# Quantising the input of two four-bit feed-forwards inside the stages ahead of them

## Chip, cores and metric

The program runs on one core of one Trainium2 chip, as one launch. The metric is the device time of the execution in microseconds (us); the profile is one execution taken by the hardware profiler. Engines go by PE (TensorE), DVE (VectorE), ACT (ScalarE), POOL (GpSimd) and SP (SyncE).

## What is computed

A stack of layers on a stream `x` of 2 x 1024 tokens with 128 features. The change is about three neighbouring ones. Each normalises its input, and the four-bit feed-forward (layer L2) rounds both factors of each product to a four-bit grid in blocks of 16 numbers:

```
def fp4_quant_dequant(x):                     # blocks of 16 along the last axis
    scale = max(|xb|) / 6 per block, at least 1e-12
    idx = searchsorted(_MID, |xb / scale|)
    return _GRID[idx] * sign(xb) * scale      # grid 0, .5, 1, 1.5, 2, 3, 4, 6
def _L2_ffn_ref(x, w_gate, w_up, w_down):     # 128 -> 352 -> 128
    h = silu(fp4_linear(x, w_gate)) * fp4_linear(x, w_up)
    return fp4_linear(h, w_down)              # fp4_linear rounds input and weight
...
x = x + 0.5 * _L1_ffn_ref(_layernorm(x), ...)     # ternary weights, 128 -> 512 -> 512 -> 512 -> 128
x = x + 0.5 * _L2_ffn_ref(_layernorm(x), ...)
x = x + _L2_attn_ref(_layernorm(x), ...)          # 16 heads, window of 32 keys
x = x + 0.5 * _L2_ffn_ref(_layernorm(x), ...)
```

## The kernel before

Tokens lie on the partitions: 16 tiles of 128 tokens, in four chunks of four tiles. `x` is the stream, `y` a normalised copy, `zt` that copy turned (features on the partitions), which the products read. The list `STAGES` runs one function per stage, each in a block of its own; in a block every engine has a queue written out by hand, and counters (semaphores) tie them. Between blocks all engines meet. Four stages matter here.

**The ternary stage** (`ternary_ffn`, with `four_bit=True`) makes the inner products of all chunks and then, chunk by chunk, the second hidden product (`pe_hidden(1, c)`, L508, closed by a Gelu on ACT, L535) and the output of the chunk before (`pe_down`, L518), which DVE scales and adds to `x` (`dve_add`, L549 and L552).

**The four-bit stage** (`l2_ffn`, run twice) makes its own input, per chunk: statistics on DVE (`dve_spread`, L3065 to L3070), a root on POOL (L3231), the normalisation, on DVE for chunk 0 (L3075) and on ACT for the others (`act_normal`, L3082 and L3087), the scaling to the grid and the exponents on DVE (`dve_x_grid`, L2952 to L2961), a step size on ACT (`act_x_step`, L3199), rounding on DVE (`dve_x_round`, L2967, L2968, L3099), four transposes on PE (`pe_turn_x`, L3160) and a copy to `zt` on ACT (L3203). Then, per tile, `pe_up` makes two products (L3171) into one of two pairs of banks, ACT gates one (`act_gated`, L3211), DVE multiplies (`dve_gated`, L3107), which frees the pair. Four tiles together are the hidden chunk, which DVE brings to the grid (`dve_hidden_grid`, begins with L3120) and rounds (`dve_hidden_round`) before PE turns it and makes the output (L3182, L3192) and DVE adds it (L3113).

**The attention stage** (`l2_attn`) between the two runs a loop over the 16 tiles. For tile n PE makes the scores (`pe_scores`, L3551 and L3556), DVE takes the maximum and subtracts it (`dve_shift`, L3620 and L3624); then PE turns the probabilities of tile n-1, makes the values and starts on the next scores, for which it waits for the subtraction. DVE meanwhile divides tile n-1 (`dve_norm`, L3631 and L3633). In tiles 5, 9 and 13 PE turns a finished chunk (L3520), in 6, 10 and 14 it makes its output (L3533), which DVE adds to `x` (`dve_add`, L3539); the next turn of probabilities waits for that add.

The order of the queues in the four-bit stage's opening is, on DVE and on PE:

```
dve_spread 0, 1; dve_normal 0; dve_x_grid 0; dve_spread 2; dve_x_round 0; dve_x_grid 1; dve_spread 3
dve_x_round 1; dve_x_grid 2; dve_gated 0; dve_x_round 2; dve_gated 1; dve_x_grid 3; dve_gated 2
dve_x_round 3; dve_gated 3; dve_hidden_grid 0 (with dve_gated 4, 5); dve_gated 6, 7; dve_hidden_grid 1
PE: pe_turn_x 0; pe_up 0, 1; pe_turn_x 1; pe_up 2, 3; pe_turn_x 2; pe_up 4, 5; pe_turn_x 3; pe_up 6 to 13
```

## Time and profile before

| | us |
|---|---|
| median of 3 runs | 2329.48 (2328.91 to 2331.28) |
| the profiled execution | 2333.61 |
| its span | 2331.8 |
| PE busy in the span | 2101.2 (90%) |
| DVE busy | 1543.0 (66%) |
| ACT busy | 1197.4 (51%) |

The span is counted from the first to the last instruction, and all times of rows from its start. Busy time is the time in which an engine executed something. A share over the whole span mixes stages with different limits, so the stretch of one stage is looked at by itself. The granted clock of PE is given as a part of 2.4 GHz; 0.50 is 1.2 GHz.

### The profile page before, as it was taken

The page shows a single profiled execution, that of the slowest core. Times are in us where ns is not written, and L with a number is a line of the kernel's source. Part 1 is how long each engine was busy: PE and PEld are TensorE (multiplying, and loading weights), DVE is VectorE, ACT ScalarE, POOL GpSimd, SP SyncE. Part 2 cuts the span into 40 slices and gives each one's busy share as a digit, 9 for nine tenths or more (in the row PEclk, how much of TensorE's full clock was granted, in tenths as well). Part 3 has the DMA queues.
Part 4 walks back from the last instruction along what each step waited for, and adds up shares of the span by engine and source line. Part 5 has one row for each costly group of instructions (what it writes and reads, how often), then busy time and mean ns, then how long its engine had stood idle before and what let it go on. Part 6 is the DMA issues. An engine that isn't in the chain of part 4 may idle for free. (4 is left out here: it accounts for less than half of the span.)

```text
span 2331.8 us, 40476 instructions
## 1 busy us (share of the span) xinstructions
PE 2101.2 (90%) x15567; PEld 1158.7 (50%) x15567; DVE 1543.0 (66%) x2999; ACT 1197.4 (51%) x2168; POOL 530.6 (23%) x896
## 2 busy tenths in 40 slices
PE   6998998796999898899999999989877957999999
PEld 3765665474675576454322222234445725445454
DVE  7996996656997897325678888350297777066650
ACT  4774773254775775222378878632143643242421
POOL 4432430313431441104154544000004010000000
PEclk9999999797999999999989999899978978999999
DMA  4000000001000000002111211000000110000000
GB/s 147 4 6 3 4 5 6 5 3 52 4 5 5 1 7 6 28 0 67 37 54 38 53 49 40 2 10 0 5 1 16 29 52 9 0 1 1 1 9 10
DMA packets 48549, 45.18 MB, mean 19 GB/s; under 512 B 33124, under 2 KB 39460, under 8 KB 47588
## 3 DMA queue, kind: packets, MB, share of 16 engines
q1 hardware_dynamic: 39252, 34.90, 5.0%
q0 software_dynamic: 9104, 7.68, 1.3%
q8 instruction: 125, 2.05, 0.4%
q14 instruction: 68, 0.56, 0.1%
HBM read 34.18 MB, written 4.46 MB: 17 GB/s over the span
## 5 line engine op out<-in xcount | busy, mean ns | idle before, releaser
L2532 DVE TENSOR_REDUCE fa_top<-psum 128x1 f32<-128x1024 f32 x256 | 300.4, 1215 | 53.3 <-PE psum L2411 52.7
L2508 ACT ACTIVATE fa_prob<-psum 128x512 f32<-128x512 f32 x512 | 274.9, 598 | 67.6 <-PE psum L2466 67.2
L758 POOL TENSOR_TENSOR turn_a<-turn_a,turn_b 128x1024 f32<-128x1024 f32 x64 | 151.3, 2364 | 268.5 <-DVE turn_b L978 268.5
L2466 PE MATMUL psum<-fa_stack_q,fa_stack_k 74*128 74x512 bf16 x512 | 160.4, 396 | 7.9 <-ACT fa_prob L2508 5.2
L2481 PE MATMUL psum<-fa_prob,fa_pair_v 128*32 128x512 f32 x1024 | 141.7, 626 | 0.0
L2366 POOL DMA_DIRECT2D area_a<-fa_parts_dram x240 | 133.5, 559 | 18.4 <-issue 18.4
L775 PE MATMUL psum<-area_a,zt 128*128 128x512 f32 x256 | 129.0, 627 | 4.5 <-ACT zt L1193 2.7
L2121 POOL TENSOR_TENSOR rstd<-spread,minus_half 128x4 f32<-128x4 f32 x20 | 20.3, 1014 | 468.3 <-DVE spread L2110 468.3
L2466 PEld LDWEIGHTS psum<-fa_stack_q,fa_stack_k 74*128 74x128 bf16 x512 | 33.8, 98 | 161.4 <-ACT fa_prob L2508 118.7
L3875 PE MATMUL psum<-hidden_a,area_b 128*128 128x512 f32 x256 | 112.5, 592 | 0.0
L3875 PE MATMUL psum<-hidden_b,area_b 128*128 128x512 f32 x256 | 111.5, 592 | 0.0
L3914 DVE TENSOR_TENSOR scaled<-psum,area_b 128x512 f32<-128x512 f32 x8 | 5.5, 692 | 138.4 <-PE psum L3884 138.4
L799 PE MATMUL psum<-ident,qk 128*128 128x128 f32 x512 | 72.3, 286 | 27.3 <-DVE turn_b L978 17.1
L991 DVE TENSOR_TENSOR qk<-turn_a,norm 128x1024 f32<-128x1024 f32 x64 | 78.4, 1225 | 27.9 <-POOL norm L750 26.3
L975 DVE TENSOR_TENSOR turn_a<-psum,direct 128x512 f32<-128x512 f32 x128 | 87.7, 685 | 7.9 <-ACT squares L881 5.9
L834 PE MATMUL psum<-ident,prob 128*128 128x128 f32 x512 | 69.7, 279 | 25.7 <-ACT prob L918 23.5
L834 PEld LDWEIGHTS psum<-ident,prob 128*128 128x128 f32 x512 | 55.4, 141 | 73.9 <-ACT prob L918 71.2
L1111 PE MATMUL psum<-glu_in,area_a 128*128 128x512 f32 (+1 forms) x192 | 88.8, 598 | 3.6 <-ACT glu_in L1098 3.6
L978 DVE TENSOR_TENSOR turn_b<-psum,cross 128x512 f32<-128x512 f32 x128 | 86.9, 679 | 0.0
L775 PEld LDWEIGHTS psum<-area_a,zt 128*128 128x128 f32 x256 | 50.5, 201 | 71.3 <-issue 53.8
L918 ACT ACTIVATE prob<-shifted_scores 128x1024 f32<-128x1024 f32 x64 | 67.6, 1057 | 33.4 <-DVE shifted_scores L1002 33.3
L2409 PE MATMUL psum<-fa_stack_k,fa_stack_q 64*128 64x512 bf16 x256 | 81.5, 385 | 2.8 <-DVE fa_top L2532 2.7
(421 smaller groups left out, 4684.4 us busy)
## 6 DMA issues: line engine op xcount, KB each, us to landing
area_b<-in_L_ffn SPq DMA_DIRECT2D x2, 2888.0 KB, 9.6
fa_stack_q<-fa_parts_dram SPq DMA_DIRECT2D x144, 32.0 KB
fa_stack_k<-fa_parts_dram SPq DMA_DIRECT2D x144, 32.0 KB
area_a<-fa_parts_dram POOLq DMA_DIRECT2D x120, 32.0 KB, 2.7
area_a<-in_L_ffn SPq DMA_DIRECT2D x1, 2482.0 KB, 18.1
moved_halves<-y SPq DMA_DIRECT2D x16, 127.0 KB
area_a<-fa_parts_dram POOLq DMA_DIRECT2D x120, 16.0 KB, 2.5
area_b<-in_L_attn SPq DMA_DIRECT2D x1, 1880.5 KB, 20.4
```

The lines of the kernel that those rows point to most:

```text
L758: nc.gpsimd.tensor_tensor(turn_a[:], turn_a[:], turn_b[:], ALU.add).then_inc(rotary_sums.handle, 1)
L775: nc.tensor.matmul(qk_banks[:, s, :], zt[:, 64 + n * P:64 + (n + 1) * P], wq[:, s * LA_INNER:(s + 1) * LA_INNER], start=True, stop=True).t ...
L834: last = nc.tensor.transpose(heads_of(prob_banks)[:, h, :], prob[:, h, :], core.ident[:])
L975: nc.vector.tensor_tensor(turn_a[:, s * H:(s + 1) * H, :], qk_banks[:, s, :].rearrange("p (h d) -> p h d", d=D), direct[:, s, t:t + 1, :]. ...
L978: last = nc.vector.tensor_tensor(turn_b[:, s * H:(s + 1) * H, :].rearrange("p h (a d) -> p h a d", a=2), partner, cross[:, s, t:t + 1, :]. ...
L1111: last = nc.tensor.matmul(pair(u)[0:rows, part, :], w(f"w1{l}")[:, part * GLU_HID + at:part * GLU_HID + at + rows], ht[:, c * CHUNK:(c + 1 ...
L2366: pool.dma_start(to[at:at + D, :, :], parts_dram[b, which, pair[which]].rearrange("(h d) t -> d h t", d=D)[:, 2 * q:2 * q + 2, tokens]).th ...
L2466: nc.tensor.matmul(slot_bank("scores", n), stack_k[0:STACK, head, t * P:(t + 1) * P], stack_q[0:STACK, head, half * CHUNK:(half + 1) * CHU ...
L2481: last = nc.tensor.matmul(psum[at:at + GROUP, SUM_BANK, :], pair_v[:, g % 2, t, j, :], prob[:, (2 * s + j) % RING, half * CHUNK:(half + 1) ...
L2508: nc.scalar.activation(prob[:, (2 * s + j) % RING, half * CHUNK:(half + 1) * CHUNK], slot_bank("scores", n), ACT.Exp, scale=float(D) ** -0 ...
L2532: nc.vector.tensor_reduce(top[:, g % 2, j, t:t + 1], psum[:, 2 * j:2 * j + 2, :].rearrange("p a n -> p (a n)"), AX.X, ALU.max, negate=True ...
L3875: last = nc.tensor.matmul(hid_bank(n), w(name)[:, e * TF_HID + m * P:e * TF_HID + (m + 1) * P], source[:, i, e, :], start=(e == 0), stop=( ...
```

## The change

A class `FourBitInput` holds the steps that make the four-bit stage's input, so that other stages can issue them. In the ternary stage DVE does the statistics and the normalisation of chunks 0 to 2 behind the adds of these chunks, and also grid and rounding of chunks 0 and 1, which PE turns there and ACT copies to `zt`. In the attention DVE does the same work between tiles (statistics in tiles 7, 11, 15, normalisation in 8, 12 and after 15, grid in 9 and 13, rounding in 10 and 14), but nothing is turned. The four-bit stage (`first_l2_ffn` with `turned=True`, `second_l2_ffn` without) keeps the statistics and normalisation of chunk 3, grid and rounding of chunks 2 and 3 and their turns, and, in its second run, the turns of chunks 0 and 1. Its queues have a new order: the turn of chunk 2 stands ahead of `pe_up(2)`, that of chunk 3 ahead of `pe_up(10)`. The diff, cut:

```diff
+        given = FourBitInput(core, ctx) if four_bit else None
...
         def act_gelu(act, step, c):
             out, scale = ((hb, "t1"), (ha, "t2"))[step]
             for m in range(M):
+                if given is not None and step and c >= 2 and m == 2:
+                    given.act_step(act, c - 2)
                 n = step * HIDS + c * M + m
...
+                if given is not None:
+                    for c in range(given.NORMAL_EARLY):
+                        given.pool_root(pool, c)
...
                     pe_hidden(pe, 1, c)
                     if 0 <= c - 2 < early:
                         following.pe_turn(pe, c - 2, psum[:, c - 2, :])
+                    if given is not None and c >= 2:
+                        if c == 2:
+                            pe.wait_ge(*guest.taken.at(4))
+                        given.pe_turn(pe, c - 2, psum[:, c - 2, :])
                     pe_down(pe, c - 1)
...
+                        if given is not None and step and c >= 2:
+                            given.act_take(act, c - 2, psum[:, c - 2, :])
...
+                    if given is not None and c < given.NORMAL_EARLY:
+                        link = Steps(dve, given.chain)
+                        dve.wait_ge(*added.at(c + 1))
+                        given.dve_spread(dve, link, c)
+                        given.dve_normal(dve, c)
+                        if c < given.EARLY:
+                            given.dve_grid(dve, link, c)
+                            given.dve_round(dve, link, c)
+                        link.close()
...
+class FourBitInput:
+
+
+    EARLY, NORMAL_EARLY = 2, 3
...
+    def dve_spread(self, dve, link, c):
+        core, nc = self.core, self.core.nc
+        for i in self.tiles(c):
+            last = nc.vector.bn_stats(core.stats[:, i, :], core.x[:, i, :])
+        link(last)
+        for i in self.tiles(c):
+            last = nc.vector.bn_aggr(core.moments[:, i, :], core.stats[:, i, :])
+        link(last)
+        nc.vector.tensor_scalar(core.spread[:, self.group(c)], core.moments[:, self.group(c), 1], 1e-5, None,
+                                ALU.add).then_inc(self.spreads.handle, 1)
...
+    def pool_root(self, pool, c):
+        core = self.core
+        pool.wait_ge(*self.spreads.at(c + 1))
+        core.nc.gpsimd.tensor_tensor(core.rstd[:, self.group(c)], core.spread[:, self.group(c)], core.minus_half[:, self.group(c)],
+                                     ALU.pow).then_inc(self.roots.handle, 1)
...
+    def dve_normal(self, dve, c):
+        core, nc = self.core, self.core.nc
+        dve.wait_ge(*self.roots.at(c + 1))
+        for i in self.tiles(c):
+            last = nc.vector.tensor_scalar(core.y[:, i, :], core.x[:, i, :], core.moments[:, i, 0:1], core.rstd[:, i:i + 1],
...
+        last.then_inc(self.whole.handle, 1)
...
+    def dve_grid(self, dve, link, c):
+        dve.wait_ge(*self.whole.at(c + 1))
+        q4_to_grid(self.core.nc, link, self.blocks(self.chunk(c)), self.blocks(self.chunk(c)), self.small[c % 2])
+        q4_exponent(self.core.nc, self.chunk(c), self.x_step[:, c % 2, :]).then_inc(self.exps.handle, 1)
...
+    def act_step(self, act, c):
+        act.wait_ge(*self.exps.at(c + 1))
+        self.core.nc.scalar.activation(self.x_step[:, c % 2, :], self.x_step[:, c % 2, :], ACT.Copy, scale=Q4_MAGIC).then_inc(self.steps.handle, 1)
...
+    def dve_round(self, dve, link, c):
+        dve.wait_ge(*self.steps.at(c + 1))
...
+                                          ALU.mult).then_inc(self.ready.handle, 1)
...
+    def pe_turn(self, pe, c, bank):
+        core, nc = self.core, self.core.nc
+        pe.wait_ge(*self.ready.at(c + 1))
+        for j, i in enumerate(self.tiles(c)):
+            last = nc.tensor.transpose(bank[:, j * P:(j + 1) * P], core.y[:, i, :], core.ident[:])
+        last.then_inc(self.turned.handle, 1)
+
+    def act_take(self, act, c, bank):
+        core, nc = self.core, self.core.nc
+        act.wait_ge(*self.turned.at(c + 1))
+        nc.scalar.copy(core.zt[:, c * CHUNK:(c + 1) * CHUNK], bank).then_inc(self.taken.handle, 1)
...
+def l2_ffn(core, area, turned):
...
-            if c == 1 and j == 0:
+            if c <= 1 and j == 0:
                 pe.wait_ge(*x_taken.at(CHUNKS))
...
-                for c in range(CHUNKS):
-                    pool.wait_ge(*spreads.at(c + 1))
-                    nc.gpsimd.tensor_scalar(minus_mean[:, group(c)], core.moments[:, group(c), 0], -1.0, None, ALU.mult).then_inc(centres.handle, 1)
-                    nc.gpsimd.tensor_tensor(core.rstd[:, group(c)], core.spread[:, group(c)], core.minus_half[:, group(c)],
-                                            ALU.pow).then_inc(roots.handle, 1)
+                pool.wait_ge(*given.spreads.at(CHUNKS))
+                nc.gpsimd.tensor_scalar(minus_mean[:], core.moments[:, group(last_chunk), 0], -1.0, None, ALU.mult).then_inc(centres.handle, 1)
+                given.pool_root(pool, last_chunk)
...
-                for c in range(CHUNKS):
-                    pe_turn_x(pe, c)
-                    if c < 3:
-                        pe_up(pe, 2 * c)
-                        pe_up(pe, 2 * c + 1)
-                for n in range(6, 14):
+                if not turned:
+                    given.pe_turn(pe, 0, psum[:, 4, :])
+                    given.pe_turn(pe, 1, psum[:, 5, :])
+                for n in range(14):
+                    if n == 2:
+                        given.pe_turn(pe, 2, psum[:, 6, :])
+                    if n == 10:
+                        given.pe_turn(pe, 3, psum[:, 7, :])
                     pe_up(pe, n)
...
-                act_normal(act, 1)
-                act_x_step(act, 0)
-                act_normal(act, 2)
-                act_take_x(act, 0)
-                act_x_step(act, 1)
+                if not turned:
+                    given.act_take(act, 0, psum[:, 4, :])
+                    given.act_take(act, 1, psum[:, 5, :])
                 act_gated(act, 0)
-                act_normal(act, 3)
-                act_x_step(act, 2)
-                act_take_x(act, 1)
                 act_gated(act, 1)
+                given.act_step(act, 2)
+                act_normal(act)
                 act_gated(act, 2)
-                act_x_step(act, 3)
-                act_take_x(act, 2)
-                act_gated(act, 3)
-                act_gated(act, 4)
-                act_take_x(act, 3)
-                act_gated(act, 5)
-                act_gated(act, 6)
+                given.act_take(act, 2, psum[:, 6, :])
+                for n in range(3, 8):
+                    act_gated(act, n)
                 act_step(act, 0)
-                act_gated(act, 7)
+                given.act_step(act, 3)
                 act_gated(act, 8)
                 act_gated(act, 9)
+                given.act_take(act, 3, psum[:, 7, :])
                 act_step(act, 1)
                 for n in range(10, 14):
                     act_gated(act, n)
...
-                dve_spread(dve, link, 0)
-                dve_spread(dve, link, 1)
-                dve_normal(dve, link, 0)
-                dve_x_grid(dve, link, 0)
-                dve_spread(dve, link, 2)
-                dve_x_round(dve, link, 0)
-                dve_x_grid(dve, link, 1)
-                dve_spread(dve, link, 3)
-                dve_x_round(dve, link, 1)
-                dve_x_grid(dve, link, 2)
+                given.dve_spread(dve, link, 3)
+                given.dve_grid(dve, link, 2)
                 dve_gated(dve, 0)
-                dve_x_round(dve, link, 2)
                 dve_gated(dve, 1)
-                dve_x_grid(dve, link, 3)
+                given.dve_round(dve, link, 2)
                 dve_gated(dve, 2)
-                dve_x_round(dve, link, 3)
                 dve_gated(dve, 3)
                 dve_hidden_grid(dve, link, 0, (4, 5))
+                given.dve_grid(dve, link, 3)
                 dve_gated(dve, 6)
                 dve_gated(dve, 7)
+                given.dve_round(dve, link, 3)
                 dve_hidden_grid(dve, link, 1, (8, 9))
...
+def first_l2_ffn(core, area):
+    l2_ffn(core, area, turned=True)
+
+
+def second_l2_ffn(core, area):
+    l2_ffn(core, area, turned=False)
...
+                for c in range(given.NORMAL_EARLY):
+                    given.pool_root(pool, c)
...
@@ -3744,6 +3798,8 @@
                         act_take_p(act, n - 1)
                     if n + 1 < TILES:
                         act_take_v(act, n + 1)
+                    if n in (10, 14):
+                        given.act_step(act, n // PER_CHUNK - 2)
                     act_exp(act, n)
...
+                later = Steps(dve, chain)
                 for n in range(TILES):
                     dve_shift(dve, n)
                     if n:
                         dve_norm(dve, n - 1)
                     if n < CHUNKS:
                         dve_keep(dve, n)
+                    if n in (10, 14):
+                        given.dve_round(dve, later, n // PER_CHUNK - 2)
                     if n > PER_CHUNK and n % PER_CHUNK == 2:
                         dve_add(dve, n // PER_CHUNK - 1)
+                    if n in (7, 11, 15):
+                        dve.wait_ge(*added.at(n // PER_CHUNK))
+                        given.dve_spread(dve, later, n // PER_CHUNK - 1)
+                    if n in (8, 12):
+                        given.dve_normal(dve, n // PER_CHUNK - 2)
+                    if n in (9, 13):
+                        given.dve_grid(dve, later, n // PER_CHUNK - 2)
+                given.dve_normal(dve, 2)
+                later.close()
                 dve_norm(dve, TILES - 1)
                 dve_add(dve, CHUNKS - 1)
...
-          ("L2_ffn", l2_ffn, 0), ("L2_attn", l2_attn, 1), ("L2_ffn", l2_ffn, 0),
+          ("L2_ffn", first_l2_ffn, 0), ("L2_attn", l2_attn, 1), ("L2_ffn", second_l2_ffn, 0),
```

PE, at the end of the ternary stage and the start of the first four-bit stage. Before (L518 outputs, L508 hidden products, L3160 turns of the input, L3171 `pe_up`):

```order
L518 MATMUL psum<-area_b,hidden_a 128x128 x16
L508 MATMUL psum<-hidden_b,area_b 128x512 x16
L518 MATMUL psum<-area_b,hidden_a 128x128 x16
L508 MATMUL psum<-hidden_b,area_b 128x512 x16
L518 MATMUL psum<-area_b,hidden_a 128x128 x32
L554 UNCONDITIONAL_BRANCH
L3234 UNCONDITIONAL_BRANCH
L3160 MATMUL psum<-ident,y 128x128 x4
L3171 MATMUL psum<-area_a,zt 128x352 x4
```

and with the change (L519, L509, L3120 and L3237 are the same four):

```order
L519 MATMUL psum<-area_b,hidden_a 128x128 x16
L509 MATMUL psum<-hidden_b,area_b 128x512 x16
L3120 MATMUL psum<-ident,y 128x128 x4
L519 MATMUL psum<-area_b,hidden_a 128x128 x16
L509 MATMUL psum<-hidden_b,area_b 128x512 x16
L3120 MATMUL psum<-ident,y 128x128 x4
L519 MATMUL psum<-area_b,hidden_a 128x128 x32
L557 UNCONDITIONAL_BRANCH
L3290 UNCONDITIONAL_BRANCH
L3237 MATMUL psum<-area_a,zt 128x352 x4
L3120 MATMUL psum<-ident,y 128x128 x4
```

Two turns now stand ahead of the outputs of chunks 1 and 2 in the ternary stage, and in the four-bit stage one turn stands between tiles 1 and 2, where there were four, the first ahead of all products.

DVE, in the attention loop, tile 10. Before:

```order
L3620 TENSOR_REDUCE wa_top<-psum 128x16
L3624 TENSOR_TENSOR wa_shifted<-psum,wa_top 128x1024
L3631 RECIPROCAL wa_rec<-psum 128x16
L3633 TENSOR_TENSOR wa_tokens<-psum,wa_rec 128x4x4x8
L3539 TENSOR_TENSOR x<-psum,x 128x512
L3620 TENSOR_REDUCE wa_top<-psum 128x16
```

and with the change, from the end of tile 9's guest on (L3672 to L3685 are L3620 to L3633 of before, L3591 is the add L3539):

```order
L2977 TENSOR_TENSOR y<-y,q_x_small_0_143 128x512
L2982 TENSOR_SCALAR q_x_step<-y 128x512
L3672 TENSOR_REDUCE wa_top<-psum 128x16
L3676 TENSOR_TENSOR wa_shifted<-psum,wa_top 128x1024
L3683 RECIPROCAL wa_rec<-psum 128x16
L3685 TENSOR_TENSOR wa_tokens<-psum,wa_rec 128x4x4x8
L2988 SCALAR_TENSOR_TENSOR y<-q_x_step,y 128x512
L2989 SCALAR_TENSOR_TENSOR q_x_step<-q_x_step,y 128x512
L3112 TENSOR_TENSOR y<-q_x_step,q_x_small_0_142 128x512
L3591 TENSOR_TENSOR x<-psum,x 128x512
L3672 TENSOR_REDUCE wa_top<-psum 128x16
```

The grid of chunk 0 stands between tile 9 and the maximum of tile 10, its rounding between tile 10's division and the add.

## Rows read from the trace of the kernel before

**Rows 1.** Windows: start:end, us, then busy us of PE, PEld, DVE, ACT, POOL, clock, DMA.
```profile
1641.30:1682.50 41.20, 38.35 (x162) 22.85 (x160) 5.53 (x8) 5.50 (x8) 0.00 (x1) 1.00 0.01 1
...
1682.50:1710.50 28.00, 14.24 (x32) 8.09 (x32) 26.16 (x80) 14.54 (x36) 7.07 (x10) 0.58 0.03 10
...
1817.10:1873.60 56.50, 50.20 (x1434) 42.81 (x1432) 35.24 (x50) 33.92 (x59) 0.00 (x0) 0.98 0.10 20
...
1874.90:1902.90 28.00, 11.19 (x32) 6.33 (x32) 26.12 (x80) 14.89 (x37) 7.21 (x10) 0.70 0.24 98
```
**Rows 2.** Timeline of DVE, first four-bit stage: start, us, instruction, count, idle before and releaser.
```profile
1682.54 0.87 DVE L3065 BATCH_NORM_STATS2 stats<-x 128x6 f32<-128x128 f32 x4 [1.43 <-PEq L4258]
...
1685.42 1.12 DVE L3075 TENSOR_SCALAR y<-x,moments,rstd 128x128 f32<-128x128 f32 x4
...
1686.58 0.69 DVE L2952 TENSOR_REDUCE q_x_small<-y 128x32 f32<-128x512 f32 x1
...
1689.19 0.86 DVE L3065 BATCH_NORM_STATS2 stats<-x 128x6 f32<-128x128 f32 x4
...
1690.58 0.68 DVE L2967 SCALAR_TENSOR_TENSOR y<-q_x_step,y 128x512 f32<-128x512 f32 x1
...
1692.63 0.68 DVE L2952 TENSOR_REDUCE q_x_small<-y 128x32 f32<-128x512 f32 x1
...
1710.54 1.62 DVE L3120 TENSOR_REDUCE q_small<-q_hidden 128x88 f32<-128x1408 f32 x1
...
1718.62 0.52 DVE L3107 TENSOR_TENSOR q_hidden<-psum,q_gate 128x352 f32<-128x352 f32 x1 [1.36 <-ACT q_gate L3211]
...
1719.18 1.62 DVE L3120 TENSOR_REDUCE q_small<-q_hidden 128x88 f32<-128x1408 f32 x1
```
**Rows 3.** Timeline of POOL, PE and ACT, first four-bit stage.
```profile
1685.70 1.04 POOL L3231 TENSOR_TENSOR rstd<-spread,minus_half 128x4 f32<-128x4 f32 x1
...
1692.77 1.12 PE L3160 MATMUL psum<-ident,y 128*128 128x128 f32 x4 [13.12 <-DVE y L3099]
...
1694.83 5.06 PE L3171 MATMUL psum<-area_a,zt 128*128 128x352 f32 x8 [0.94 <-ACT zt L3203]
...
1695.35 0.63 ACT L3199 ACTIVATE q_x_step<-q_x_step 128x512 f32<-128x512 f32 x1 [0.57 <-DVE q_x_step L2961]
...
1701.85 1.45 PE L3171 MATMUL psum<-area_a,zt 128*128 128x352 f32 x4 [1.16 <-DVE q_hidden L3107]
```
**Rows 4.** Windows in the opening of the first four-bit stage (clock third from the end).
```profile
1686.00:1700.00 14.00, 6.29 (x14) 3.79 (x15) 13.24 (x43) 10.28 (x28) 4.98 (x5) 0.50 0.00 1
...
1700.00:1704.00 4.00, 2.14 (x8) 1.02 (x6) 3.60 (x7) 2.51 (x6) 0.00 (x0) 0.93 0.00 0
...
1704.00:1710.00 6.00, 5.31 (x12) 3.27 (x12) 5.50 (x13) 1.58 (x3) 0.00 (x0) 0.50 0.00 0
```
**Rows 5.** Timeline of PE and DVE, end of the ternary stage.
```profile
1641.30 13.90 PE L508 MATMUL psum<-hidden_b,area_b 128*128 128x512 f32 x32
...
1679.69 0.69 DVE L549 TENSOR_TENSOR scaled<-psum,area_b 128x512 f32<-128x512 f32 x1 [2.16 <-PE psum L518]
```
**Rows 6.** Timeline of PE and DVE, attention loop and its end.
```profile
1819.35 0.66 PE L3520 MATMUL psum<-ident,wa_tokens 128*128 128x128 f32 x4
...
1835.32 1.22 DVE L3620 TENSOR_REDUCE wa_top<-psum 128x16 f32<-128x1024 f32 x1 [1.30 <-PE psum L3556]
...
1839.71 1.22 DVE L3620 TENSOR_REDUCE wa_top<-psum 128x16 f32<-128x1024 f32 x1 [1.34 <-PE psum L3556]
...
1843.19 0.69 DVE L3539 TENSOR_TENSOR x<-psum,x 128x512 f32<-128x512 f32 x1 [0.45 <-PE psum L3533]
...
1844.71 1.22 DVE L3620 TENSOR_REDUCE wa_top<-psum 128x16 f32<-128x1024 f32 x1 [0.82 <-PE psum L3556]
...
1868.95 0.26 DVE L3631 RECIPROCAL wa_rec<-psum 128x16 f32<-128x16 f32 x1 [3.06 <-PE psum L3592]
```
**Rows 7.** Timeline of DVE, second four-bit stage, its second hidden grid.
```profile
1911.56 1.62 DVE L3120 TENSOR_REDUCE q_small<-q_hidden 128x88 f32<-128x1408 f32 x1
```

More of the change, by code:

```diff
@@ L3096, in dve_x_round @@
[L3096 to L3100 removed]
+            last.then_inc(given.whole.handle, 1)
         def dve_gated(dve, n):
```

98 lines of the change are left out of this document (40 added, 58 removed).

## The prediction, made before the changed kernel had run

> **What bounds the kernel now.** I first read the windows, one per stretch of the four stages that the change touches [rows 1]; in each the reader is to see which engine is full. In the last 41.2 us of the ternary feed-forward TensorE is busy for 38.35 us at full clock and VectorE for 5.53: TensorE is the bound and VectorE has room. The opening of the first four-bit stage turns that round: in 28.0 us VectorE is busy for 26.16 and TensorE for 14.24, and the second four-bit stage opens alike (26.12 of 28.0). What ends last there is VectorE's own queue, so work taken out of it shortens the opening until another wait ends last. In the windowed attention both are nearly full (TensorE 50.20, VectorE 35.24 of 56.5 us), so there I went on to the timeline: between tiles VectorE waits 1.34 us for the next scores [rows 6]. That gap is all the free room the guests find there.
>
> **What is taken out of a four-bit stage.** From the starts of VectorE's instructions [rows 2]: the statistics of a chunk take 1.39 us (1689.19 to 1690.58), its normalisation 1.16 (1685.42 to 1686.58), scaling to the grid with the exponents 2.61 (1686.58 to 1689.19), rounding with the last multiply 2.05 (1690.58 to 1692.63). Gone from each stage are three statistics (4.2), one normalisation (1.16), two grids (5.2) and two roundings (4.1): 14.7 us of VectorE's 28. ScalarE loses its normalisation of chunks 1 and 2, which VectorE never waited for.
>
> **What the opening then waits for.** I lay it out anew, counting from VectorE's first instruction. The prices are these [rows 3]: a tile's products take TensorE 2.53 us at the low clock (5.06 for eight instructions, two tiles) and 1.45 at the high one, four transposes 1.12 low (0.66 high [rows 6]), a step on ScalarE 0.63; a gate product on VectorE is 0.56 with its gap [rows 2]. VectorE does chunk 3's statistics and chunk 2's grid up to 4.0. TensorE starts at 0.1, since `zt` is filled, and is cold: tile 0 is made at 2.6, tile 1 at 5.1. ScalarE's gate of tile 1, half a us, ends at 5.65 and VectorE's product at 6.2: a first stall of about 1.1. The step of chunk 2 ends at 6.3, its rounding at 8.35. Only now can TensorE turn chunk 2, and in its queue tiles 2 to 13 stand behind that turn, though tiles 2 and 3 lie in chunk 0 and need nothing of it. So VectorE idles again: transposes to 9.5, tiles 2 and 3 to 14.5, last product over at 15.6 if TensorE stays cold; with the high clock from 8.35 on, 13.0. The hidden grid began at 28.0 before (1710.54) [rows 2].
> From there to the second hidden grid it was 8.64 us, 1.36 of them a wait for ScalarE [rows 2], which the new ScalarE order takes away; chunk 3's grid and rounding are added: 7.28 + 2.61 + 2.05 = 11.94. The second hidden grid begins at 25.0 (warm) or 28.5 (cold, with 1 us for tiles 4 and 5, whose products come every 2.53) instead of 36.64. Later the order is unchanged, and chunk 3's turn, which now stands ahead of tile 10, has its input at that moment, 8 us before the product is wanted: nothing. Gain 8.1 to 11.6; I take **10.0**, since the clock was granted at 0.93 for 4 us and at 0.50 around it [rows 4]: neither end holds throughout.
> The Trainium skill ("TensorE: Matmul & The Clock Gate", section "What's actually happening") says that half clock is the default state and activity releases it; with a pause of 3.3 us ahead of the turn I read it as the cold end for both openings, 2323.1 us, a rival below. The trace sides with it only in part, since there is a high clock in a half idle opening [rows 4].
>
> The **second four-bit stage** has to turn chunks 0 and 1 itself: two turns of 1.12 ahead of tile 0, with the first copy hidden under the second turn. All of the chain above moves back by 2.2 us. Its old opening had the same length (36.66 us from 1874.90, where its window begins, to its second hidden grid at 1911.56) [rows 1, 7]. Gain 5.9 to 9.4; I take **7.9**.
>
> **What the ternary stage pays.** TensorE is the bound there, and gets 2 x 4 transposes, 0.66 each four at full clock [rows 6]: +1.3. The inputs are there in time: between chunk 0's output and its turn stands a hidden product of 13.9 us [rows 5], and the chain on VectorE, add and all (1.4 + 1.4 + 1.1 + 1.2 + 2.6 + 0.7 + 2.1), is 10.5; chunk 1 likewise. ScalarE's steps and copies lie in its gaps between two Gelus. After chunk 2's add VectorE has 2.16 us until chunk 3's product [rows 5]; now 1.39 + 1.04 (root on GpSimd [rows 3]) + 0.1 + 1.16 = 3.7 stand there ahead of chunk 3's product and add, with which the stage ends: +1.5. Together **+2.8** (1.3 if the last part hides, 3.4 with a slower root).
>
> **What the attention pays.** Its loop is a ring: scores on TensorE, maximum and subtraction on VectorE, next scores. Guests stand in VectorE's gap of 1.34 [rows 6]. Statistics (tiles 7, 11) exceed it by 0.06, normalisations (8, 12) fit, grids (9, 13) exceed it by 1.27 each. In tiles 10 and 14 the add leaves 0.45 + 0.82 = 1.27 [rows 6] for a rounding of 2.05, and the add is now late for the turn that waits for its bank: 0.8 each. After tile 15 VectorE waits 3.06 for the values [rows 6]; statistics, root and normalisation are 3.7: +0.6. Sum 0.1 + 2.5 + 1.6 + 0.6 = **+4.8**. Below, 3.1, if only grids and the tail count; above, 9.8, if the two statistics and two normalisations find no gap either (2 x 1.39 + 2 x 1.16). I stay with the rows of the gap. ScalarE's step ahead of an exponential (0.63) delays a turn that comes 1 us later: nothing. GpSimd's roots stand behind its last DMA issue, long done; SyncE's queue is untouched.
>
> **Sum**: -10.0 - 7.9 + 2.8 + 4.8 = -10.3 us. The profiled execution took 2333.6 (span 2331.8), 4.1 above the median of the runs, 2329.5; taken off that median: **2319.2**.
>
> **Rivals.**
> 1. TensorE stays at the low clock through both openings: -8.1 - 5.9 + 7.6 = -6.4, 2323.1. For it: 0.50 over most of the first opening [rows 4]. Against: 0.93 in between, and 0.70 as the mean of the second [rows 1].
> 2. The attention ring has no gap at all and pays all 17.0 us of its guests (4.2 + 3.5 + 5.2 + 4.1): -17.9 + 2.8 + 17.0 = +1.9, 2331.4. Against: the 1.34 us in each tile.
> 3. The moved work isn't what opened late: TensorE and ScalarE give back half of the gain. -9.0 + 7.6 = -1.4, 2328.1. Against: VectorE busy for 93% of the openings.
> 4. Slower: the attention's clock falls. VectorE's grid in tile 9 leaves TensorE idle for 1.3 us more; if that takes the clock from 2.4 to 1.2 GHz for the seven tiles to the end, each costs its 3.9 us of TensorE work (a tile each 4.39, 1835.32 to 1839.71, 89% of it busy [rows 1, 6]) times 0.74 (0.63 us cold over 0.36 warm for one product instruction [rows 3]), 2.9 us: -10.3 + 20.3 = +10.0, **2339.5**. It outweighs the gain from the fourth slow tile on. Against: over 56.5 us the clock is 0.98, the tail with its 3.06 us of waiting in it [rows 1, 6]. The Trainium skill, on the same page under "HAM oscillation — how this bites in real kernels", shows a matmul loop that goes back to half clock in each wait between tiles, which would be this rival; the trace has not yet shown such a wait to be long enough.
>
> **How the numbers follow.** The forecast has 0.67, rival 1 0.17, rivals 2 and 3 0.05 each, rival 4 0.06. 0.2% is 4.7 us, about what a measurement of this kernel can tell from no change. Forecast and rival 1 are faster by more (0.84), rivals 2 and 3 within it (0.10), rival 4 slower (0.06). With all terms at their good ends the sum is -11.6 - 9.4 + 1.3 + 3.1 = -16.6, 2312.9; at their bad ends -14.0 + 3.4 + 9.8 = -0.8, 2328.7. Not all end at one side together; the range 2314 to 2326 holds the forecast with most of both and rival 1, and leaves out rivals 2 to 4 and the outermost corners.
>
> **What would show it.** In the new profile the first hidden grid should start 13 to 16 us after the first four-bit stage's first instruction and 15 to 18 after the second's, with TensorE's largest wait there the turn of chunk 2 behind VectorE's rounding. The ternary stage should be 2.8 us longer and the attention 4.8, seen as starts of the maximum 5.6 instead of 4.4 us apart after tiles 9 and 13. The prediction is wrong if the hidden grid starts after 20 us, if the attention's granted clock leaves 1.00 ahead of its tail, or if the rest of either four-bit stage, from its second hidden grid on, grows by over 1 us.

## The result, and the profile after

| | before | after |
|---|---|---|
| median, us | 2329.22 (2328.91 to 2331.28, 4 runs) | 2313.01 (2312.36 to 2316.81, 4 runs) |
| the profiled execution | 2333.61 | 2312.74 |
| its span | 2331.8 | 2310.9 |
| PE, DVE, ACT busy | 2101.2, 1543.0, 1197.4 | 2095.6, 1548.3, 1188.1 |

The ratio is 0.9932, 95% interval 0.9916 to 0.9947: 16.2 us faster where 10.3 were forecast, and 1 us below the range. DVE's work is the same sum as before to 0.4% (1543.0 and 1548.3 us busy); what changed is where it is done. I cut both traces into stages, each from DVE's first statistics instruction behind the block's start to the next stage's (the full attention and the ternary stage begin at their table load on ACT). In the last column is a second profile of the kernel before, the experiment e1 below.

| stage, us | before | after | before, again (e1) |
|---|---|---|---|
| full attention (untouched) | 387.86 | 380.75 | 382.18 |
| ternary feed-forward | 164.64 | 167.04 | 164.64 |
| first four-bit stage | 84.17 | 73.29 | 85.27 |
| to its first, second hidden grid | 28.00, 36.64 | 13.27, 24.99 | 28.01, 36.66 |
| from there on | 47.53 | 48.30 | 48.61 |
| windowed attention | 108.25 | 114.28 | 109.52 |
| second four-bit stage | 85.20 | 74.63 | 85.15 |
| to its first, second hidden grid | 27.96, 36.60 | 15.70, 27.41 | 27.97, 36.61 |
| from there on | 48.6 | 47.2 | 48.5 |

The four touched stages together went from 442.3 us to 429.2. This is 13.0 less; against the second profile of before, 444.6, it is 15.3 less.

First the windows of the changed kernel that answer to [rows 1] (start:end, us, then busy us of PE, PEld, DVE, ACT, POOL, granted clock, DMA share, GB/s): the last 38 us of the ternary stage, the first opening, the same tiles of the attention as in [rows 1], and the second opening.

```profile
1640.05:1678.05 38.00, 33.61 (x156) 21.14 (x155) 18.11 (x50) 7.04 (x12) 2.04 (x3) 1.00 0.01 1
...
1678.05:1706.05 28.00, 19.69 (x47) 10.98 (x48) 22.15 (x45) 11.05 (x23) 1.58 (x4) 0.76 0.03 9
1802.04:1863.50 61.46, 51.37 (x1432) 43.45 (x1431) 49.95 (x106) 35.39 (x61) 3.05 (x3) 0.97 0.10 20
1865.60:1893.60 28.00, 19.62 (x49) 11.71 (x50) 19.87 (x42) 11.70 (x24) 1.57 (x4) 0.74 0.23 97
```

DVE has 18.11 us of work at the end of the ternary stage instead of 5.53, and still PE is what is full there. In the openings DVE's load fell from 26 us of 28 to 22.15 and 19.87, and PE's rose from 14.24 and 11.19 to 19.7 and 19.6. Before, the 28 us ended with the first hidden grid; now they reach past the start of the second in both stages. In them the two engines take turns. The clock of the openings is 0.76 and 0.74; it was 0.58 and 0.70. In the attention the same tiles went from 56.5 us to 61.46, and DVE from 35.24 us busy to 49.95, 81% of the stretch.

DVE in the first opening, timeline of the changed kernel (start, us, instruction, count, idle before and releaser), which answers to [rows 2]:

```profile
1678.06 0.87 DVE L3078 BATCH_NORM_STATS2 stats<-x 128x6 f32<-128x128 f32 x4 [1.44 <-PEq L4326]
...
1682.89 0.52 DVE L3181 TENSOR_TENSOR q_hidden<-psum,q_gate 128x352 f32<-128x352 f32 x1 [0.31 <-ACT q_gate L3269]
...
1684.86 0.69 DVE L3112 TENSOR_TENSOR y<-q_x_step,q_x_small 128x512 f32<-128x512 f32 x1
1689.59 0.52 DVE L3181 TENSOR_TENSOR q_hidden<-psum,q_gate 128x352 f32<-128x352 f32 x1 [4.04 <-ACT q_gate L3269]
1690.78 0.52 DVE L3181 TENSOR_TENSOR q_hidden<-psum,q_gate 128x352 f32<-128x352 f32 x1 [0.66 <-ACT q_gate L3269]
1691.33 1.62 DVE L3194 TENSOR_REDUCE q_small<-q_hidden 128x88 f32<-128x1408 f32 x1
...
1703.05 1.61 DVE L3194 TENSOR_REDUCE q_small<-q_hidden 128x88 f32<-128x1408 f32 x1
```

and PE beside it:

```profile
1678.06 4.30 PE L3237 MATMUL psum<-area_a,zt 128*128 128x352 f32 x8 [4.40 <-PEq L4326]
1685.61 1.12 PE L3120 MATMUL psum<-ident,y 128*128 128x128 f32 x4 [3.25 <-DVE y L3112]
1686.52 6.35 PE L3237 MATMUL psum<-area_a,zt 128*128 128x352 f32 x16
```

The last step of chunk 2's rounding begins at 1684.86. PE, idle for 3.25 us, turns the chunk at the low clock (1.12 us for four), and only then makes tiles 2 and 3, for which DVE has waited 4.04 and 0.66 us. The hidden grid starts 13.27 us into the stage. That is the new wait the prediction described; it is the largest piece of idle time of DVE in the opening, and it invites an experiment (e4). In the second opening DVE waits for its third and fourth product 4.05 and 1.78 us.

### The profile page after: what moved, and what is told of

Same layout as the page of the kernel before. It is cut to its first block and busy times, and to the rows that moved or that the text cites. A ratio compares the mean times of both kernels' runs of the same rounds, so it can differ in the third digit from the quotient of the medians.

```text
span 2310.9 us, 40447 instructions
## 1 busy us (share of the span) xinstructions
PE 2095.6 (91%) x15567; PEld 1161.9 (50%) x15567; DVE 1548.3 (67%) x3015; ACT 1188.1 (51%) x2136; POOL 526.7 (23%) x890
```

## The experiments

Times of one set are compared with runs of the kernel before in that set: 2331.51 us for e1 to e4, 2332.33 for e5 to e8, 2331.0 for e9 and e10.

**e1: the kernel before, again.** No edit. The stage that the change doesn't touch, the full attention, was 7.1 us shorter in the profile of after. Is that chance?

> The kernel before, once more, for its profile. In the first two profiles the stages ahead of the ternary one, which the change does not touch, took 6.9 us less with the change (DVE and PE code there is the same), nearly all in the long full attention (387.9 against 380.8 us between its last table load and the ternary stage's). Theory A, chance of the granted clock: this profile's full attention can lie anywhere between 380 and 390, and so can those of the next three kernels, whose code up to there is the same too. Theory B, the change shortens it in some way: this profile has about 388 again and kernels with the new parts about 381. Time the same as before.

Measured: 2331.2 us, ratio 0.9998 (0.9989 to 1.0006), the full attention 382.18 us. A window at the full attention's end, in the profile of before:

```profile
1480.00:1518.00 38.00, 31.49 (x158) 8.77 (x155) 2.44 (x9) 22.43 (x44) 0.86 (x4) 0.82 0.02 3
```

and in e1, the same program, whose full attention ends 5.6 us earlier:

```profile
1474.70:1512.70 38.00, 29.85 (x180) 8.78 (x178) 5.61 (x16) 25.95 (x51) 1.71 (x8) 1.00 0.02 5
```

The granted clock was 0.82 at the end in one execution and 1.00 in the other. All twelve profiles of this study sort by this: the first profile of before and that of e4, a changed kernel, had 0.82 over the stage's last 38 us and took 387.9 and 387.6 us for it; the other ten had 1.00 and took 380.8 to 382.7. Two programs, that of before and that of e4 and e10, are in both groups. So it is chance, and not a gain of the change; what decides the clock there stays open. The 20.9 us between the two profiled spans therefore overstate the change, and the touched stages have to be compared by themselves.

**e2 and e3: one half of the change each.** The old functions, kept under other names, run in the stages that the edit leaves as before.

```diff
 e2
-          ("L2_ffn", first_l2_ffn, 0), ("L2_attn", l2_attn, 1), ("L2_ffn", second_l2_ffn, 0),
+          ("L2_ffn", first_l2_ffn, 0), ("L2_attn", old_l2_attn, 1), ("L2_ffn", old_l2_ffn, 0),
 e3
-        given = FourBitInput(core, ctx) if four_bit else None
+        given = None
...
-          ("L2_ffn", first_l2_ffn, 0), ("L2_attn", l2_attn, 1), ("L2_ffn", second_l2_ffn, 0),
+          ("L2_ffn", old_l2_ffn, 0), ("L2_attn", l2_attn, 1), ("L2_ffn", second_l2_ffn, 0),
```

> The change in the ternary stage and the first four-bit stage alone; attention and second four-bit stage as before. By the stage times of the two profiles: ternary stage +2.4, first four-bit stage -10.9, so -8.5 us (-7.2 by the prediction's terms, +2.8 and -10.0). If the two pairs are independent, this and the second pair sum to the whole.

> The change in the attention and the second four-bit stage alone. By the stage times of the profiles: attention +6.0, second four-bit stage -10.6, so -4.6 us (-3.1 by the prediction's terms, +4.8 and -7.9). If both pairs together fall short of the measured 16.2 us by about 3, that rest lies in the untouched stages.

Measured: e2 2321.02 us, ratio 0.9959 (0.9947 to 0.9972), 9.6 us; e3 2324.18, 0.9974 (0.9963 to 0.9984), 6.1 us. The two shares add up to 15.7, and the whole change's 0.9932 gives 15.8 (a second measurement, e5, gives 0.9921, 18.4 us). Within the intervals the halves add up, and each pays. Of e2's stages only its own pair differs from e1's: ternary 167.05, first four-bit 73.24. In e3 the second opening was 2.9 us shorter than in the changed kernel, with the same instructions in it: 24.47 to its second hidden grid against 27.41. PE in that opening of the changed kernel, timeline:

```profile
1874.46 1.12 PE L3120 MATMUL psum<-ident,y 128*128 128x128 f32 x4 [3.25 <-DVE y L3112]
1875.37 7.42 PE L3237 MATMUL psum<-area_a,zt 128*128 128x352 f32 x16
```

and of e3:

```profile
1886.12 0.66 PE L3120 MATMUL psum<-ident,y 128*128 128x128 f32 x4 [3.25 <-DVE y L3112]
1886.62 5.16 PE L3237 MATMUL psum<-area_a,zt 128*128 128x352 f32 x16
```

The pause of PE is the same 3.25 us, and behind it the clock was low in one execution and high in the other. This order was profiled in eight openings (the changed kernel, e2, e3, e5, e7): in seven the turn took 1.11 or 1.12 us and the 16 instructions behind it 6.26 to 7.47, in e3 alone 0.66 and 5.16.

**e4 and e10: the turn of chunk 2 four tiles later.** PE makes tiles 2 to 5, whose input lies in chunks 0 and 1, before it turns chunk 2; ACT copies it after gate 5. In the changed kernel PE's queue holds these tiles behind a turn that they don't need.

```diff
 (pe)
-                    if n == 2:
+                    if n == 6:
                         given.pe_turn(pe, 2, psum[:, 6, :])
...
 (act)
-                act_gated(act, 2)
-                given.act_take(act, 2, psum[:, 6, :])
-                for n in range(3, 8):
+                for n in range(2, 6):
                     act_gated(act, n)
+                given.act_take(act, 2, psum[:, 6, :])
+                act_gated(act, 6)
+                act_gated(act, 7)
```

> The change with the turn of chunk 2 ahead of tile 6 rather than tile 2 in both four-bit stages (ScalarE's copy moved likewise). My theory: VectorE's waits of 4.04 and 4.05 us ahead of its third product come from TensorE standing at that turn until the rounding is done; they go, and by the second hidden grid 3 to 4.7 us are won per stage, less what TensorE's pace at the low clock (about 2.4 us a tile) takes back: -6 to -9 us against the change in all. Rival: TensorE and ScalarE would be late for tiles 2 to 7 in any case (low clock, 2.4 us per tile), the wait only moves to tiles 4 to 7, and less than 2 us are won.

> The same program as e4_turn_late, a second time, beside e9. Theory (its gain over the change is the wait for ScalarE's gating that VectorE no longer has in its order, in both openings): 2306.7 again within 1.5, ratio to before 0.989, the two four-bit stages at 68.9 and 70.7 us within 0.7. Rival (part of it was a run with fewer falls of the clock): 2309 to 2311, and the two stages at 70 to 72.

Measured: e4 2306.73 us, ratio 0.9893 (0.9878 to 0.9909); e10, the same program, 2308.43, 0.9907 (0.9894 to 0.9921). The stages are 68.93 and 70.71 us in e4, 68.99 and 70.65 in e10, where the change had 73.29 and 74.63: 4.3 and 4.0 less. By the medians it is 6.3 and 4.6 less than the change's 2313.01, and e8 below, which has this edit too, is 4.5 less than the changed kernel beside it (e5). So the theory of e4 holds: 8.3 us by the two stages and 4.5 to 6.3 by the medians, where 6 to 9 were expected. The median of e10 is 0.2 us outside what was expected of it, its two stages are within 0.1. PE in the first opening of e10, timeline:

```profile
1679.88 4.09 PE L3237 MATMUL psum<-area_a,zt 128*128 128x352 f32 x8 [4.41 <-PEq L4327]
1684.46 2.63 PE L3237 MATMUL psum<-area_a,zt 128*128 128x352 f32 x8 [0.48 <-DVE q_hidden L3181]
1688.58 2.60 PE L3237 MATMUL psum<-area_a,zt 128*128 128x352 f32 x8 [1.49 <-DVE q_hidden L3181]
1691.03 0.60 PE L3120 MATMUL psum<-ident,y 128*128 128x128 f32 x4
```

and DVE:

```profile
1686.48 0.69 DVE L3112 TENSOR_TENSOR y<-q_x_step,q_x_small 128x512 f32<-128x512 f32 x1
1687.91 0.96 DVE L3181 TENSOR_TENSOR q_hidden<-psum,q_gate 128x352 f32<-128x352 f32 x2 [0.74 <-ACT q_gate L3269]
1688.90 1.62 DVE L3194 TENSOR_REDUCE q_small<-q_hidden 128x88 f32<-128x1408 f32 x1
```

DVE waits 0.74 us where it waited 4.7, and the hidden grid starts at 9.02. In this opening PE has no pause over 1.5 us up to the turn, and its clock is high from tile 2 on: eight product instructions take 2.63 us, not 5.06 as in [rows 3], and the turn 0.60, not 1.12. The wait of 0.74 is found in the first opening of e4 too; the early clock isn't: there the first 16 instructions took 7.63 us, and the hidden grid started at 9.96. So the gain that repeats is DVE's wait; whether the order also brings a better clock isn't shown.

**e5 and e6: how much of the opening is the clock.** e5 is the changed kernel again; e6 has twelve transposes of the identity, whose output nobody reads, in PE's pause ahead of chunk 2's turn.

```diff
                     if n == 2:
+                        for k in range(12):
+                            nc.tensor.transpose(psum[:, 6, (k % 4) * P:(k % 4 + 1) * P], core.ident[:], core.ident[:])
                         given.pe_turn(pe, 2, psum[:, 6, :])
```

> The change once more, for a second profile. If the untouched full attention lies anywhere between 380 and 390 us by the clock's chance, it can do so here as well. Of the touched stages, the ternary one repeats to 0.1 us (167.0), the first four-bit stage within 1.5 (73.3), the attention within 1.5 (114.3), and the second four-bit stage within 3 (74.6): its opening reached the second hidden grid after 24.5 us in the run with the second pair alone and after 27.4 in the first profile, with the same instructions, which I put down to TensorE's clock there. Time about 2313.

> The change with twelve extra transposes of the identity ahead of chunk 2's turn in each four-bit stage, into the bank that the turn then overwrites, while TensorE waits 3.25 us for the rounding. Theory, the pause lets the clock fall and tiles 2 to 5 then run at half rate: with TensorE kept busy the granted clock stays high, the first hidden grid begins at about 12.7 us in both stages (13.3 and 15.7 in the first profile), and 1 to 4 us are won in all. Rival, the clock there is set by what came before the pause, or by chance: no gain, and up to 1 us lost a stage where the twelve run at half rate (3.4 us, about as long as the pause).

Measured: e5 2313.46 us, ratio 0.9921 (0.9909 to 0.9933), stages as the change's within 0.3 us (73.31, 113.99, 74.83). e6 2312.59, 0.9919 (0.9907 to 0.9931). PE of e6, first opening, timeline:

```profile
1683.67 1.47 PE L3298 MATMUL psum<-ident 128*128 128x128 f32 x12
1687.08 0.66 PE L3120 MATMUL psum<-ident,y 128*128 128x128 f32 x4 [1.94 <-DVE y L3112]
1687.57 5.16 PE L3237 MATMUL psum<-area_a,zt 128*128 128x352 f32 x16
```

With its pause filled PE turns chunk 2 in 0.66 us and makes the tiles behind it in 5.16, not 6.35: this opening is 1.8 us shorter to the first hidden grid (11.44), the second 2.7 (13.02). So the low clock behind PE's pause costs the changed kernel 1.8 and 2.7 us in its openings. With the pause filled the clock held in both openings, left empty it held in one of eight (e3's, whose first hidden grid came at 12.74): the pause makes the fall likely, not certain. The whole kernel gained 0.9 us by the medians, nothing that can be told from zero, where 1 to 4 were expected. The stages show where: e6's ternary stage was 0.7 us longer than e5's, its attention too, and both later parts of the four-bit stages 48.5 and 48.4 against 48.3 and 47.2. What these are is seen at e7.

**e7 and e8: the attention's add ahead of the guest's rounding.**

```diff
-                    if n in (10, 14):
-                        given.dve_round(dve, later, n // PER_CHUNK - 2)
                     if n > PER_CHUNK and n % PER_CHUNK == 2:
                         dve_add(dve, n // PER_CHUNK - 1)
+                    if n in (10, 14):
+                        given.dve_round(dve, later, n // PER_CHUNK - 2)
```

> The change with the attention's add ahead of the guest's rounding in tiles 10 and 14. In the first profile TensorE's turn in tile 11 waited 1.56 us for that add and then ran at a low clock (eight transposes in 1.88 us instead of 1.09), and the maximum of tile 12 came 5.99 us after that of tile 11 instead of 4.41 before. Theory: it is the add behind the rounding; with the add first this distance is back at 4.4 to 4.5 and the stage wins about 1.6 us (only part at tile 14, where the tail hides it). Rival: the rounding itself delays the maximum and so the whole ring, the add's place is free; less than 0.5 us. The time is -1.6 or 0 against the change.

> Late turn of chunk 2 and add ahead of the rounding together. If they are independent, their gains add: the late turn alone measured 2306.7, so about 2305 here, the attention near 112.5 us and both four-bit stages near 69 and 70.5.

Measured: e7 2316.36 us, ratio 0.9934 (0.9922 to 0.9946), by the medians 2.9 slower than e5 beside it, with intervals that overlap; e8, with e4's edit too, 2308.99, 0.9904 (0.9891 to 0.9917), where 2305 was expected, no faster than e4 or e10. Yet in tile 11 the edit did what was expected. Timeline of PE in tile 11 of the changed kernel:

```profile
1829.51 1.12 PE L3608 MATMUL psum<-wa_k_rows,wa_q_rows 32*128 32x64 f32 x32
1832.19 1.88 PE L3632 MATMUL psum<-ident,wa_prob 128*128 128x128 f32 x8 [1.56 <-DVE x L3591]
1834.00 1.12 PE L3618 MATMUL psum<-area_b,zt 128*64 128x64 f32 x16
```

and of e7:

```profile
1831.22 1.12 PE L3608 MATMUL psum<-wa_k_rows,wa_q_rows 32*128 32x64 f32 x32
1832.27 1.10 PE L3632 MATMUL psum<-ident,wa_prob 128*128 128x128 f32 x8
1833.30 0.69 PE L3618 MATMUL psum<-area_b,zt 128*64 128x64 f32 x16
```

In the changed kernel the turn of the probabilities waits 1.56 us for the late add, and the clock falls behind the wait: 1.88 us for eight transposes, not 1.10. From the start of tile 11's maximum to that of tile 12's it takes 5.99 us there (5.62 in e5), and 4.41 in e7. What e7 won there, 1.2 to 1.6 us, it lost in two other places: ahead of its first maximum, where it has no edit, and at the end, behind tile 14, where it has one. Windows of the changed kernel (10 us after the attention's start, and the last 3.5 us ahead of the second four-bit stage):

```profile
1761.35:1766.35 5.00, 5.00 (x12) 2.34 (x11) 2.71 (x9) 0.78 (x1) 1.94 (x2) 0.73 0.01 3
...
1862.13:1865.63 3.50, 1.33 (x8) 1.06 (x9) 0.69 (x1) 0.00 (x0) 0.04 (x1) 0.62 0.39 86
```

and of e7, the same places:

```profile
1762.50:1767.50 5.00, 5.00 (x9) 2.39 (x8) 2.70 (x9) 0.78 (x1) 1.94 (x2) 0.50 0.01 3
...
1863.79:1867.29 3.50, 1.34 (x7) 1.07 (x6) 0.69 (x1) 0.00 (x0) 0.04 (x1) 0.50 0.31 73
```

At the attention's start the same instructions met a clock that rose a little later, 0.50 instead of 0.73, and the first maximum came 1.2 us later. Nothing points to the edit there: in e4, without it, the first maximum came as late. The end, from the last maximum on, took 13.71 us in e7 instead of 12.18. There the edit joined two waits of PE, of 1.56 and 1.17 us, into one, timeline of e7:

```profile
1857.28 1.97 PE L3632 MATMUL psum<-ident,wa_prob 128*128 128x128 f32 x8 [2.77 <-ACT wa_prob L3652]
```

Behind it the clock was low, in e8 as well (1.97 us for the eight, 1.09 where it is high). The ternary stage's 0.7 us is of the same kind: over its first ten us the clock was 0.66 in the changed kernel, e2, e4, e5 and both profiles of before, and 0.50 or 0.51 in e6 to e10, whose ternary stages took 167.7 to 167.8 us with the same instructions. And the later parts of the four-bit stages took either 47.2 to 47.7 or 48.2 to 48.6 us in all executions, of every version and of the kernel before alike. I read this as a lot of about a microsecond at each place where PE comes out of a pause, some six times in these stages; what decides it no run here shows. A second lot lies in the transfers: in some profiles PE waits 0.6 to 1.5 us in one or a few tiles of the attention for its query rows from DMA (1.09 in tile 7 of the changed kernel, 0.97 in tile 11 of e1). An edit worth 1.2 us doesn't show through them.

**e9: the guests' last rounding multiply on POOL**, e4's edit included.

```diff
                     if n in (10, 14):
-                        given.dve_round(dve, later, n // PER_CHUNK - 2)
+                        given.dve_round_short(dve, later, n // PER_CHUNK - 2)
...
+    def pool_scale(self, pool, c):
+        pool.wait_ge(*self.rounded.at(c + 1))
+        self.core.nc.gpsimd.tensor_tensor(self.blocks(self.chunk(c)), self.blocks(self.x_step[:, c % 2, :]),
+                                          self.small[c % 2][1].unsqueeze(2).to_broadcast([P, CHUNK // Q4_BLOCK, Q4_BLOCK]),
+                                          ALU.mult).then_inc(self.ready.handle, 1)
```

> The late turn (e4_turn_late), and in the attention the guests' last rounding multiply goes from VectorE to GpSimd, so that the add behind it in VectorE's order starts 0.6 us sooner. Theory (the price of the second chunk's rounding in the attention is the place it takes in VectorE's order ahead of the add): each of the tiles 10 and 14 loses 0.6 us, the stage of the attention becomes 112.2 instead of 113.4, the sum 1.2 us less than e4_turn_late in the same call, near 2305.5. Rival (GpSimd's multiply comes between GpSimd's own steps of the rounding and hands the 0.6 us on, or slows VectorE beside it): no difference, 2306.7 within 1.5, and the turn of tile 14's probabilities still waits over 1 us for VectorE.

Measured: 2304.62 us, ratio 0.9895 (0.9879 to 0.991), beside e10's 2308.43 and 0.9907. Timelines of e9 in tile 10, one row each of DVE, POOL and PE:

```profile
1829.64 0.68 DVE L3606 TENSOR_TENSOR x<-psum,x 128x512 f32<-128x512 f32 x1
...
1829.80 1.06 POOL L3126 TENSOR_TENSOR y<-q_x_step,q_x_small 128x512 f32<-128x512 f32 x1 [13.82 <-DVE q_x_step L3121]
...
1830.47 1.06 PE L3647 MATMUL psum<-ident,wa_prob 128*128 128x128 f32 x8 [0.85 <-DVE x L3606]
```

POOL's multiply takes 1.06 us beside DVE's add, which is as short as ever (0.68). The distances from tile 10 to 11 and from 14 to 15 are 4.88 us each, 5.61 in e10: 0.7 twice, where the theory had 0.6. That add reads one operand from PSUM; how it fares with two in SBUF no run here shows. PE waits 0.85 us instead of 1.57, and no fall of the clock follows in tiles 11 and 15. The attention stage took 111.77 us, 113.65 in e10, 1.9 less where 1.2 was expected. By the medians e9 is the fastest of all versions; by the intervals e9, e4 and e10 can't be told apart.

## Why the prediction was wrong, by its steps

The direction and the places of gain and loss were as predicted; the sum was 6 us too small and the range ended 1 us above the result. Of the 6, by the table, the openings have 3.0, the later parts of the four-bit stages 1.6 and the ternary stage 0.4; the rest, 0.9, is what stages and medians differ by. Against e1's profile, which stands nearer to the median of before, the stages give:

| term | predicted | measured |
|---|---|---|
| first four-bit stage | -10.0 (-11.6 to -8.1) | -11.7 to its second hidden grid, -0.3 later |
| second four-bit stage | -7.9 (-9.4 to -5.9) | -9.2 to its second hidden grid, -1.3 later |
| ternary stage | +2.8 (1.3 to 3.4) | +2.4 |
| attention | +4.8 (3.1 to 9.8) | +4.8 |
| sum | -10.3 | -15.3 |

**The openings: the term that failed.** "I take **10.0**, since the clock was granted at 0.93 for 4 us and at 0.50 around it" and, for the second, "I take **7.9**". The step that failed is this choice of a middle between two ends, and behind it the prices of the low end: PE at the low clock for tiles 0 and 1, the turn, and tiles 2 and 3 (5.06 + 1.12 + 5.06), and 1 us for tiles 4 and 5. Windows of the changed kernel, of the first eight product instructions and of what follows:

```profile
1678.06:1682.36 4.30, 4.30 (x8) 2.15 (x8) 4.06 (x16) 1.71 (x2) 1.57 (x4) 0.60 0.18 57
...
1682.00:1686.00 4.00, 0.75 (x3) 0.39 (x3) 3.17 (x6) 3.42 (x10) 0.00 (x0) 0.93 0.01 2
1686.00:1690.00 4.00, 4.00 (x12) 2.47 (x10) 0.41 (x1) 0.90 (x2) 0.00 (x0) 0.64 0.00 0
1690.00:1694.00 4.00, 3.28 (x11) 1.75 (x11) 3.24 (x6) 1.43 (x4) 0.00 (x0) 1.00 0.00 0
```

Counted from each stage's first instruction, in us:

| | low end | high end | first opening | second opening |
|---|---|---|---|---|
| chunk 2 rounded (predicted 8.35 and 10.55) | | | 7.49 | 8.78 |
| from there to the first hidden grid | 7.25 | 4.65 | 5.78 | 6.92 |
| from there to the second hidden grid | 12.94 | 11.94 | 11.72 | 11.71 |

Tiles 0 and 1 took 4.30 us, and 3.82 in the second opening, since the clock had left 0.50 before they were done; so the input was rounded 0.9 and 1.8 us sooner. By the end of the pause the clock had fallen, and the turn took 1.12. It came back within the products behind it: 6.35 us for 16 in the first opening, 7.42 in the second, where the high clock gives 5.16 (e3 and e6) and the low one 10.1 (twice the 5.06). And tiles 4 and 5 cost nothing of their own. The old opening, whose clock I had carried over, had PE busy for half of the time in short pieces [rows 1, 3]; the new one has a run, a pause and a longer run. Both openings came out within 0.2 us of their good ends (11.7 for 11.6, 9.2 for 9.4), but by different ways, and how near is partly luck: with the same order other executions reached the second hidden grid at 24.96 to 25.93 us in the first stage, and at 24.47 (e3) to 27.60 (e5) in the second, where 24.47 lies beyond the good end.

**The later parts.** They had no term, since their order is unchanged, and -1.6 us stand there in this comparison. Against the first profile of before it is -0.6 (+0.8 and -1.4). The lot that the runs show at this place (47.2 or 48.5 us) can't be predicted, but it belongs in a range.

**The range.** "Not all end at one side together" was the wrong step: both openings were reckoned with the same prices, of tiles 0 and 1 and of 4 and 5, so an error in these moves both openings to the same side, and the two had to be added as one. And I made the sum against one profiled execution whose touched stages were 2.3 us short of e1's, while its untouched one was long; what made that execution 4.1 us longer than the median lay outside the stages that the change touches, in the full attention above all. What is left, from 15.3 to the medians' 16.2, is within the interval of the ratio.

**The ternary stage: right.** Each turn took 0.60 us, for 0.66, and the inputs were there; DVE's product of chunk 2's output came 0.9 us later in the stage. From there to that of chunk 3 it is 5.09 us instead of 3.58, the +1.5 of the prediction. At its end the normalisation of chunk 2 stands ahead of chunk 3's product, and waits for its root, timeline of DVE:

```profile
1674.18 1.11 DVE L3096 TENSOR_SCALAR y<-x,moments,rstd 128x128 f32<-128x128 f32 x4 [1.12 <-POOL rstd L3089]
1675.21 0.68 DVE L552 TENSOR_TENSOR scaled<-psum,area_b 128x512 f32<-128x512 f32 x1
```

**The attention: right in its parts, with one missed, and lucky in its exact sum.** The +4.8 is against e1, whose attention had a wait for DMA of 0.97 us in it; against the first profile of before it is +6.0. The three profiles with the old attention took 108.3 to 109.5 us, the six with the new one and the late add 113.4 to 115.4. The grids cost 1.17 and 1.18 us (5.56 from maximum to maximum instead of 4.39 and 4.38), 1.27 predicted. Rounding and add cost 0.60 each in their own tile, 0.8 predicted. For the late add I had put nothing beyond these. What it costs shows in the tile behind: 0.1 where the clock holds (e4, 4.51 us from tile 11 to 12), 1.2 to 1.6 where it falls (5.57 in e10, 5.62 in e3, e5 and e6, 5.99 in the first profile). The wait was the same 1.56 or 1.57 us in all six. The tail's 0.6 came too, at its place: PE's last turn waits for the division, which stands behind the normalisation. Timeline of before and of the changed kernel:

```profile
1869.59 0.66 PE L3520 MATMUL psum<-ident,wa_tokens 128*128 128x128 f32 x4 [0.72 <-DVE wa_tokens L3633]
...
1860.81 0.66 PE L3572 MATMUL psum<-ident,wa_tokens 128*128 128x128 f32 x4 [1.35 <-DVE wa_tokens L3685]
```

In the length of the tail (12.11 and 12.18 us) it is hidden, since the last output product behind it took 1.87 us in the one and 1.33 in the other. Tails with the late add took 12.2 to 14.0 us in all, those of the old attention 11.4 to 12.2.

One of the prediction's signs of being wrong did appear: the attention's granted clock left 1.00 ahead of the tail, in tile 11 (0.78 and 0.79 over the 8 us from 1830). It cost that tile 1.6 us and was not what made the sum wrong, which erred to the other side.

**The rivals.** Rival 1 (low clock through both openings) is refuted by the windows above and by 6.35 and 7.42 us for 16 instructions. Rival 2 (the ring pays 17.0) by +4.8 to +6.0. Rival 3 (half of the gain given back) was right in its place, the 4.7 us of DVE's new waits, but they were already in the forecast's own chain. Rival 4 (the attention's clock falls for good) happened for a single tile: 1.12 us for 16 small products in tile 11, not 0.69, and the high clock was back in the next. The Trainium skill ("TensorE: Matmul & The Clock Gate", section "HAM oscillation — how this bites in real kernels") describes a loop that falls to half clock in each wait between tiles; the page puts these waits, for DMA, at 3 to 5 us. The wait of 1.56 us here is shorter, and by the runs it is in between: in tile 11 of six executions with it the clock fell in five, and behind the same wait in tile 15 in four of six.

## What to carry to other kernels

When work leaves the engine that bounds a stage's opening, look next at what the following engine holds in its queue behind a step that it doesn't need: moving one turn four tiles back was worth another 4 us in each stage (4.5 to 6.3 in the whole kernel), on top of the 11 that the change had brought there. Don't carry a clock from the old order to a new one without asking how PE's runs and pauses change, and when the range is made treat all terms that rest on one price as one. Compare stages, not spans, and profile the kernel before twice: chance in a stage that nobody touched was 7 us here, half of the effect.

## What was not expected of the hardware

A stage of some 382 us whose code is the same in all programs took between 380.8 and 387.9 us in the profiled executions; the two longest, 387.6 and 387.9, had a granted clock of 0.82 over the last 38 us, the ten others 1.00. A wait of 1.57 us of PE made the clock fall in some executions of one program and not in others (8 transposes in 1.06 us in e4, and in e10 1.20, with 16 small products at 1.12 us instead of 0.69 behind them). A pause of 3.25 us was followed by a low clock in seven openings and by a high one in the eighth; with twelve transposes that nobody needed, 1.47 us, in it, the clock was high behind it in both openings of e6. POOL's multiply of 128x512 with a broadcast operand, 1.06 us, left DVE's add beside it at its usual 0.68.
